# Eight steps' x parts from 49 block products of 96 columns in place of two times 7 of 192, in a GRU whose TensorE has no idle time

## What is computed

```python
def step(H, xs):
    xz, xr, xh = xs                       # X @ W.T + b for all steps, from x alone
    Z = sigmoid(xz + H @ Whz.T + bhz)
    R = sigmoid(xr + H @ Whr.T + bhr)
    H_tilda = tanh(xh + R * H @ Whh.T + bhh)
    H_new = Z * H + (1.0 - Z) * H_tilda
    Y = H_new @ Whq.T + bhq
    return (H_new, Y)
x = x + transpose(scan(step, h0, (Xz, Xr, Xh)))
```

## Time and profile before

| | |
|---|---|
| runs | 2152.09, 2149.66, 2150.19 us, median 2150.19 |
| profiled execution, span | 2148.1 us |
| PE matmul busy | 2141.7 us (100%) |
| DVE, ACT, GpSimd busy | 1625.9, 914.6, 167.6 us |
| granted TensorE clock | 1.00 over the whole span |
| DMA | 62.20 MB, 29 GB/s |

### The profile page before, as it was taken

How to read it: one execution, slowest core, us unless ns; L and a number is a source line. 1 busy time by engine, 2 the same in 40 slices (tenths; PEclk the granted TensorE clock), 3 DMA queues, 4 the chain that set the end, 5 groups by cost and what they waited for, 6 DMA issues and landing times.

```text
span 2148.1 us, 179447 instructions
## 1 busy us (share of the span) xinstructions
PE 2141.7 (100%) x78028; PEld 2128.3 (99%) x78028; DVE 1625.9 (76%) x9472; ACT 914.6 (43%) x5118; POOL 167.6 (8%) x524
## 2 busy tenths in 40 slices
PE   9999999999999999999999999999999999999999
PEld 7999999999999999999999999999999999999998
DVE  5777777777777777777777777777777777777777
ACT  3444444444444444444444444444444444444443
POOL 1000000000000000000000000000000000000000
PEclk9999999999999999999999999999999999999999
DMA  4100010001000000000000100010001000010000
GB/s 155 29 24 24 26 29 24 24 24 31 24 24 24 29 26 24 24 26 29 24 24 26 29 24 24 25 30 24 24 24 30 25 24 24 26 29 24 24 26 27
DMA packets 111618, 62.20 MB, mean 29 GB/s; under 512 B 28786, under 2 KB 110834, under 8 KB 110834
## 3 DMA queue, kind: packets, MB, share of 16 engines
q1 hardware_dynamic: 111600, 61.98, 9.8%
q10 hardware_dynamic: 4, 0.02, 0.0%
HBM read 45.17 MB, written 16.78 MB: 29 GB/s over the span
## 4 chain that ended last, share of the span: by engine, by line
PE 99%; DMA 0%; DVE 0%; issue 0%; ACT 0%; POOL 0%; SPq 0%; DVEq 0%; POOLq 0%
PE gates L417 62%; PE p_bank L339 15%; PE gates L339 12%; PE y_bank L347 9%; PE p_bank L448 0%; PE gates L547 0%; DMA y_io<-in_x_res 0%; PE y_bank L540 0%; PE p_bank L540 0%; DMA out<-y_io 0%; DVE scanned L708 0%; DVE pre_t L644 0%; DVE wq_sums L698 0%; DVE y_io L648 0%; ACT scan_on L629 0%
## 5 line engine op out<-in xcount | busy, mean ns | idle before, releaser
L417 PE MATMUL gates<-wh,scanned 128*16 128x128 f32 x32768 | 1009.6, 273 | 1.5 <-DVE scanned L708 1.5
L417 PEld LDWEIGHTS gates<-wh,scanned 128*16 128x16 f32 x32768 | 933.4, 104 | 3.8 <-DVE scanned L708 1.3
L644 DVE STREAM_TRANSPOSE pre_t<-gates 128x32 f32<-128x32 f32 (+2 forms) x3584 | 617.1, 216 | 183.8 <-PE gates L417 139.3
L417 PE MATMUL gates<-wh,reset_state 128*16 128x128 f32 (+1 forms) x16384 | 562.0, 273 | 0.2 <-issue 0.2
L417 PEld LDWEIGHTS gates<-wh,reset_state 128*16 128x16 f32 (+1 forms) x16384 | 445.1, 103 | 0.5 <-issue 0.3
L614 ACT ACTIVATE r_gate<-pre_t 128x16 f32<-128x16 f32 (+1 forms) x1536 | 234.5, 215 | 408.4 <-DVE pre_t L644 408.4
L629 ACT ACTIVATE scan_on<-pre_t 128x16 f32<-128x16 f32 (+1 forms) x1536 | 236.4, 218 | 263.9 <-DVE pre_t L644 263.9
L339 PE MATMUL p_bank<-t,s 128*32 128x192 f32 x6096 | 333.9, 326 | 0.3 <-issue 0.3
L708 DVE TENSOR_TENSOR_SCAN scanned<-scan_by,scan_on 128x32 f32<-128x32 f32 x2048 | 299.3, 208 | 28.5
L617 ACT ACTIVATE scan_by<-pre_t 128x64 f32<-128x64 f32 x512 | 143.0, 279 | 263.9 <-DVE pre_t L644 263.9
L769 DVE TENSOR_TENSOR scan_on<-z_gate,scanned 128x64 f32<-128x64 f32 x512 | 120.8, 236 | 173.8 <-ACT z_gate L618 173.8
(11 more groups left out here) (77 smaller groups left out, 1538.5 us busy)
## 6 DMA issues: line engine op xcount, KB each, us to landing
y_io<-in_x_res SPq DMA_DIRECT2D x256, 64.0 KB, 1.9
out<-y_io SPq DMA_DIRECT2D x256, 64.0 KB, 1.6
xr<-in_x_t SPq DMA_DIRECT2D x127, 128.0 KB, 2.0
x_b<-in_x_t SPq DMA_DIRECT2D x127, 32.0 KB, 1.7
wx_v<-in_w_xv SPq DMA_DIRECT2D x1, 1536.0 KB, 6.5
wx_u<-in_w_xu SPq DMA_DIRECT2D x1, 1536.0 KB, 9.0
wh<-in_w_hr SPq DMA_DIRECT2D x1, 1024.0 KB, 10.7
wh<-in_w_hz SPq DMA_DIRECT2D x1, 1024.0 KB, 13.8
```

The costliest lines, as they stand in the source:

```text
L417: mm = nc.tensor.matmul(gate_rows(g, par, slice(Q * j, Q * j + rows)), of, w, start=False, stop=(m == G - 1), skip_group_check=True)
L644: nc.vector.transpose(flat(pre_t[g][:, a:b]), gate_part(g, par, a, b)).then_inc(done, 1)
```

## The change

A turn now has eight steps (`s8` = 0 to 7, still four pairs of steps), and there are 64 turns. Their x parts are one product of block matrices of 4 by 4, made by the scheme of 7 applied twice: 7 products of the outer scheme (`a` = 1 to 7), each from 7 inner block products (`b`), 49 in all. Each block product is 4 matmuls of 96 columns (`x_products`): 196 matmuls in eight steps, where there were 112 of 192 columns. The recurrence (384 matmuls of 128 columns in eight steps) and the outputs (112 of 64) stay as they were.

- The inner products are made for three inner blocks (`FIRST`, 288 columns) in steps 4 to 7 of a turn, and for the other four (`SECOND`, 384 columns) in steps 7 to 4 of the next. ACT copies sums from bank to bank and out to SBUF (`a_to_b`, `d_to_c`, `z11_first` and so on, 288 or 384 columns each) and puts finished parts into the banks of the gates (`put_u`, 256 columns, and `put_v`, 128). DVE adds four times in a turn (`z22_first`, `z12_first`, `z22_second`, `z12_second`), and no longer has the five `put_...` sums that it had in four steps.
- GpSimd sums what goes in (4 sums of 128 columns, `x_sum`, and 4 of 224, `x_sub_sum`) and what comes out (`combine`: 14 sums of 96 columns and 7 of 2 x 96). That is 29 instructions in eight steps, where there were 8 of 64 columns. None of them waits for `z_turned` or `state_ready` any more, only for its data and for the room that it writes to.
- The parts made in turns n and n + 1 are used in turn n + 2. So the first 16 steps get their x part from plain products (`plain`: 6144 columns a pair of steps, in the gaps of turns 0 and 1), and the last eleven gaps have no x products at all. The sums of weights that the inner products need are made in turns 0 and 1 by DVE (`sub_sum`, 21 sums of 384 columns, and `w_t4`) and GpSimd (`w_t3` and `w_sub3`, 11 of 384).
- R's columns now lie side by side in PSUM, and Z's sums of both pairs share one bank, `v_bank`.

The core of the difference (POOL is GpSimd):

```diff
-                    pool.wait_ge(state_ready[N - 1], 4 * i + 2)
-                    sum_1(i + 1)
-                    pool.wait_ge(z_turned, 4 * i + 2)
-                    sum_2(i + 1)
-                    pool.wait_ge(z_turned, 4 * i + 3)
-                    sum_3()
-                    pool.wait_ge(z_turned, 4 * i + 4)
-                    sum_4(i + 1)
+            def combine(op, made, z, x, k):
+                pool.wait_ge(made, 7 * k + op - 1) if op > 1 or not isinstance(k, int) or k > 0 else None
+                of = {1: (x(0, 0), z(1), z(2)), 2: (z(6), z(1), z(6)), 3: (z(3), z(5), z(3)),
+                      4: (x(0, 1), z(6), z(3)), 5: (z(7), z(6), z(7)), 6: (x(1, 0), z(7), z(4)),
+                      7: (x(1, 1), z(7), z(5))}[op]
+                nc.gpsimd.tensor_tensor(*of, ALU.add).then_inc(made, 1)
...
+                if begins:
+                    x_sub_sum(1, n)
+                if ends:
+                    combine_x2(1, n - 1)
+                    combine_x2(2, n - 1)
+                if begins:
+                    x_sub_sum(2, n)
+                if ends:
+                    combine_x2(3, n - 1)
+                    combine_x2(4, n - 1)
+                    combine_21(1, n - 1)
+                if begins:
+                    x_sub_sum(4, n)
+                    x_sub_sum(3, n)
+                if ends:
+                    combine_x2(5, n - 1)
+                    combine_21(2, n - 1)
...
+            def x_products(to, a, blocks, only=None):
+                x, w = X_OF[a], W_OF[a]
...
+                    for j in range(G):
+                        mm = nc.tensor.matmul(to[Q * j:Q * (j + 1), BLOCK * at:BLOCK * (at + 1)], of, by[:, j, :],
+                                              start=False, stop=True, skip_group_check=True)
...
+                    if s8 == 4 and ends:
+                        pe.wait_ge(z22d_out, n)
+                        x_products(d_bank, 4, SECOND).then_inc(p4d_done, 1)
+                    if s8 == 4 and begins:
+                        pe.wait_ge(a_started, n + 1)
+                        pe.wait_ge(x_loaded, 16 * (n + 1))
+                        x_products(a_bank, 1, FIRST).then_inc(p1a_done, 1)
+                    elif s8 == 5 and begins:
+                        pe.wait_ge(b_put_a, n + 1)
+                        pe.wait_ge(s_ready[2], n + 1)
+                        x_products(a_bank, 6, FIRST).then_inc(p6a_done, 1)
+                        x_products(b_bank, 2, FIRST).then_inc(p2a_done, 1)
```

More of the change, by code:

```diff
@@ L576, in copy_q1, with put_u @@
                 nc.scalar.copy(y_bank[:, Y_AT[0]:Y_AT[0] + YW], y_bank[:, Q16_AT:Q16_AT + YW]).then_inc(yv_a_put, 1)
[L578 to L593 removed]
+            def put_u(par, values):
+                nc.scalar.copy(u_bank[par][:, 0:RH], values[:, 0:RH]).then_inc(u_put[par], 1)
@@ new lines, in turn @@
+            def turn(n, ends=True, begins=True):
+                static = isinstance(n, int)
+                first = static and n == 0
+                last = not ends
+                ends = ends and not first
+                for s8 in range(8):
+                    odd, c = divmod(s8, 4)
+                    i, t = 2 * n + odd, 8 * n + s8
+                    par, s = divmod(c, 2)
+                    mine = slice(B * s, B * (s + 1))
+                    p = s8 // 2
+                    end = last and odd == 1
+                    if s == 0 and (not static or n >= 2):
+                        put_v(par, x_part(p, n))
+                    if s == 0 and static and 1 <= 4 * n + p < 7:
+                        if 4 * n + p > 0:
+                            act.wait_ge(plain_done, 4 * n + p)
+                        put_u(1 - par, bias_rows)
+                        put_v(1 - par, bias_rows)
+                    if s8 == 0 and ends:
+                        p5_out_first(n - 1)
+                        d_to_b(n - 1)
+                    elif s8 == 1 and ends:
+                        d_to_c(n - 1)
+                    elif s8 == 2 and ends:
+                        z11_second(n - 1)
+                    elif s8 == 3 and ends:
+                        z21_first(n - 1)
+                    elif s8 == 4 and ends:
+                        p5_out_second(n - 1)
+                    if s8 == 5 and begins:
+                        a_to_b(n)
+                    if s8 == 5 and ends:
+                        z21_second(n - 1)
+                    if s8 == 6 and begins:
+                        a_to_c(n)
+                    elif s8 == 7 and begins:
+                        z11_first(n)
+                        start_b_a(n)
+                    if c == 2:
+                        if first and odd == 0:
@@ L712, in renew, with turn @@
                 mm.then_inc(state_ready[h], 1)
-            def turn(i, first, last):
-                for c in range(4):
-                    t = 4 * i + c
+            def turn(n, ends=True, begins=True):
+                static = isinstance(n, int)
+                first, second = static and n == 0, static and n == 1
+                last = not ends
+                ends = ends and not first
+                for s8 in range(8):
+                    odd, c = divmod(s8, 4)
+                    i, t = 2 * n + odd, 8 * n + s8
                     par, s = divmod(c, 2)
+                    end = last and odd == 1
+                    begin = first and odd == 0
                     old = state_before(c)
-                    if c == 0 and not first:
+                    if c == 0 and not begin:
                         state_sums(i)
-                    elif c == 1 and not first:
-                        put_ub(i)
-                    elif c == 2 and first:
+                    elif c == 2 and begin:
                         dve.wait_ge(q6_done, 1)
```

888 lines of the change are left out of this document (576 added, 312 removed).

## The result

The changed kernel takes 3013.2 us (median of four runs, 3008.9 to 3014.8) for 2150.9 of the kernel before: ratio 1.4006, 95% interval 1.3986 to 1.4026. The prediction was 2204, in a range of 2124 to 2265. 862 us is nine times what its largest term held, so I read the page of the changed kernel first for something that the prediction had not looked at.

The account below looks back on a forecast made before the run. TensorE bounds the kernel, with about 0.1 us to spare at two places a step. Terms -62 + 7 + 5 + 6 + 98 = +54 on the profiled 2148.1 give 2202, as a median 2204; range 2124 to 2265 us.

Parts of the forecast that it names:

- the price of TensorE's instructions: TensorE over the run: 0.6 ns for each of 10,640 more instructions, +6.4 us.
- the five rivals: Alternative outcomes for the whole kernel's time, from 2106 to 2320 us; chances 0.60, 0.23, 0.07, 0.08 and 0.02.
- Columns, -62: TensorE over the run: 163,584 fewer x product columns, -68.2 us, with more instructions at +6.4; sum -62 us.
- Ends: Last eleven gaps, without x products: eight more steps set by their chain, each losing 0.9 us of TensorE time; +7 us.
- weight sums: Turns 0 and 1: 32 sums of 384 columns on DVE and GpSimd, partly hidden; +5 us.
- gaps by step: From H to the next R, in steps 1 and 4: 0.1 us lost a turn over 61 turns; +6 us.
- GpSimd beside DVE, +98: Resets, `kept` and scans: GpSimd's sums hold DVE at a shared SBUF read interface, 1.6 us a turn; +98 us.
- Rival 2: Resets, `kept` and scans of steps 4 to 6: slack swallows the meetings with GpSimd; 2106 to 2143 us; chance 0.23.
- ACT's queue (rival 4): Odd steps: `put_u`, between r's and z's sigmoids, waits for GpSimd's counts; 2258 to 2320 us; chance 0.08.

Follow-up runs that it names:

- after: The changed kernel itself, with its loop of eight steps, against the kernel before; 3013.2 us, ratio 1.4006.
- a_flat: The changed kernel written out without a loop on every engine; 2629.8 us.
- b_flat: The kernel before written out without a loop on TensorE, DVE, ScalarE and GpSimd; 2362.5 us.
- a_less: The changed kernel with TensorE's loop for four steps, branches to the x products, half of y's and a quarter of Z's matmuls left out; 2298.7 us.
- b_split84: The kernel before with each x product of 192 columns given as two, with 84 of each 96 columns; 2131.0 us.
- b_less: The kernel before with half of y's and a quarter of Z's matmuls left out; 2065.3 us.
- b_gp_free: The kernel before with ten more GpSimd sums of 96 columns a turn of four steps, in two trains of five; 2159.0 us.
- b_pair: The kernel before with two turns (eight steps) in the loop body, nothing else changed; 2567.6 us.

## Why the prediction was wrong

**The step that failed** is the price of TensorE's instructions: "5,320 more matmuls or 10,640 instructions cost +6.4". It counted matmul instructions over the run, and never all instructions of a pass of the loop, which go from 1,217 to 2,768. A term was missing altogether, that of fetching TensorE's code anew, and none of the five rivals had it. Of 862 us, the jump back with its slow clock holds 383 (after less a_flat). In straight code the change is 267 over b_flat, 252 of it in stops at issue; b_flat pays 214 for 602 blocks that the looped kernel before doesn't load. 383 + 267 + 214 is 864, the whole, since each difference begins where the last one ends. a_less shows the same in one step: with its code kept, and a tenth of TensorE's columns left out, the changed kernel takes 2299 us.

*Columns, -62.* Right in kind and near in size. The price of a column holds, since b_split84's shortfall lies at the head of a pass; a matmul instruction costs 1.03 ns where the record had 0.6. With 10,640 of them the term is -68 + 11, some -57, an estimate from these runs. The stop at the head of a pass was not in the sum: 60 passes at b_split84's 0.3 us would be +18.

*Ends, weight sums, gaps by step (+7, +5, +6).* Not tried; hidden in the rest.

*GpSimd beside DVE, +98.* The kind was right and the size of the right order. With scans and resets as long in the mean as after has them, stand-ins whose code is kept paid 48 and, without the stops at the head of a pass, 61 us. Where TensorE has slack of its own, the changed kernel paid 233 over b_less, 0.46 us for each of 512 steps; this includes the 52 us at issue, ScalarE's copies and whatever TensorE can't gain in a kernel that its chain bounds. Rival 2, that the slack swallows it, has b_gp_free for it alone.

*ACT's queue (rival 4).* No wait on `put_u`, `b_put_a` or `x_sub_made` is among after's.

With its code kept, the whole change would be near 2150 - 57 + 18 + 18 and 48 to 61 for the hold, some 2180 to 2190, an estimate by the stand-ins. That is near the number on record, though a_less speaks for more. Whole and with kept code it was not run: no version of its body here came under the edge without leaving work out. No version here that computes everything beats the kernel before.

## What to carry to other kernels

Count TensorE's instructions in a loop body (four for each float32 matmul here) before anything else of a change: up to 1,665 they were fetched once, from 1,728 on in every pass, at 0.35 us or more a block of 256 and 3.3 us (b_pair over b_flat) to 6.4 us (after over a_flat) a jump back. A body that doesn't fit runs better written out than looped (2630 for 3013), but a body that fits beats both. Read the instruction queue's packets and "issue" in the chain first, and together: a_less has 5% of "issue" with no packets, and that isn't fetching.

## What the hardware did that I had not expected

- A loop body of 1,728 TensorE instructions was fetched whole in each pass, about 9 blocks for 6.75, while 1,665 were kept.
- Straight code costs TensorE 0.35 us a block of 256 instructions when it has no idle time otherwise; it goes on only 1.4 us after the block has landed.
- A jump forward inside kept code was free (2149.8 for 2149.7). A body of about 1,780 instructions that isn't kept, with branches and twice the passes, was 884 us slower than the longer body with no branch (3897 for 3013).
- The jump back of a kept body was free behind products of 192 columns, and stopped TensorE for 0.12, 0.29 and 0.32 us a pass behind products of 96, 84 and 64.
- Announcing the jump back gave 145 of the 383 us that it cost.
